# Column sums of the context added on the vector engine, and the order of three queues at the end of the first stage

## The chip, the cores and the metric

The kernel runs on one core of a Trainium2 chip. A core has a matrix engine (PE), a vector engine (DVE), a scalar engine (ACT), a general engine (POOL) and a queue that issues transfers (SP). Each runs its own list of instructions in order, and they wait for each other by semaphores. The metric is the time of one execution in microseconds (us) on the device; less is better.

## The reference, cut to what matters

Four steps update x (2 batches of 512 tokens, 1024 features): a product with the context, both operands rounded to 8 bits; an 8-bit feed-forward; an attention over the context; a 4-bit feed-forward. The change touches the first:

```python
def fake_quant(x, scale, zp):
    q = jnp.clip(jnp.round(x / s + z), QMIN, QMAX)
    return (q - z) * s
q1 = fake_quant(x1, x1_scale, x1_zp)
q2 = fake_quant(x2, x2_scale, x2_zp)
return jnp.matmul(q1, q2)
...
x = x + jnp.tanh(g_xattn[0]) * _L0_xattn_ref(_layernorm(x, axis=-1), ctx_4096, ...)
```

The zero points make a product with a correction: since q1 - z1 = u + (128 - z1), where u is what the kernel multiplies, the result is u times the rounded context, plus (128 - z1) times the sum of the rounded context over its 1024 tokens, for each feature (the column sums), plus a term for each token.

## The kernel before

**Stage 1** (to about 109 us) works through the 16 context tiles (128 tokens by 1024 features), in four chunks of four. Each tile is split in two fp16 halves, turned, and multiplied with Wk and Wv (v_proj, k_proj on PE). The raw tile is also scaled and clipped on POOL (ctx_affine) and rounded by DVE into `r2[:, u, :]` (ctx_round, L1043), integers in fp16 in the tile regR. In between DVE scales the eight rows of the int32 weight (wd_scale, L1049), PE turns them (wd_turn, L1463), ACT and DVE evict them in two halves (wd_high L690, wd_low L1036). The LayerNorm of x goes tile by tile (t = 0 to 7) from chunk 1 on: stats (L1058) and ln1_affine (L1065 to L1111, eight operations on two elements a partition) on DVE, a square root (L695) and the affine into `y` (L702) on ACT, ln1_round (L1115) on DVE, ln1_out (L709) on ACT, a turning transfer xt1 (L283) from SP into `xT_hi`.

**Column sums.** After the last k_proj and the turn of weight row 7, `c2_sum(n)` multiplies `ones16` with the eight rounded tiles of batch n // 2, 512 columns at a time: four sums of eight products (L1545), into bank n. ACT evicts each (c2_out, L743), and POOL adds the row to each tile of x (add_c2, L510). add_c2(0) waits for two evictions; add_c2(1) also waits until all eight roundings ln1_round are done (`ln1_q` = 8). POOL then goes on with the low halves of Wq (split_lo, L521 and L523), the bias (L530) and so on. SP loads the next row of Wq into `wraw` when such a low half is done; ACT makes the high half (wq_high, L843).

**The A/B stage** (116 to 200 us): for each tile of x the A product (16 products of 512 columns, L1612) and the B product (32, L1615 and L1616), in the order of `AB_OPS`: a0 to a4, b0, a5, b1, a6, b2, a7, b3 to b7. Three pairs of banks turn; product i waits until DVE has evicted product i - 3 (ab_out, L1216). The second, a1, also waits for `k_lo`, the low half of the last K block (k_low on DVE, L1119, behind k_out on ACT, L716), whose bank it takes. After A of a tile DVE takes the statistics, ACT the deviation from the mean (ln2_deviation, L812), DVE the largest absolute value (ln2_reduce, L1232), ACT scales and rounds (L817, L825), DVE clips (ln2_clip, L1254).

The order of each queue is written out by hand; the block of each engine is one list. `d()` is a drain on DVE: the next instruction starts when what is before it has ended.

## Time and profile before

| | us |
|---|---|
| median of 3 runs | 847.38 |
| lowest and highest | 844.66, 848.0 |
| the profiled execution | 841.13 |
| its span in the trace | 839.3 |
| PE, DVE, ACT, POOL busy | 818.1, 583.8, 449.6, 535.6 |

The profiled execution is one run of its own. The page has the busy time of each engine, the span in 40 slices, the DMA queues, the chain of work that ended last, and the costliest groups of instructions. In the rows below, L1043 is line 1043 of the kernel before. A row of an engine in order of time gives start and duration in us, engine, line, operation, output and input tiles (buffer numbers left out; mpair and sbank are banks of the accumulation memory), shapes, how many in a row, and in brackets the idle time before it and what ended it. PE's granted clock is 1.00 in all stretches used here, the higher of its two levels.

### The profile page before, as it was taken

How to read it: one execution, taken by the hardware profiler on the slowest of the kernel's cores; microseconds unless marked ns; L12 is line 12 of the kernel's file. 1: busy time of each engine (PE TensorE's matmuls, PEld its weight loads, DVE VectorE, ACT ScalarE, POOL GpSimd, SP SyncE). 2: the span in 40 equal slices, each digit the busy share in tenths (PEclk: the TensorE clock that was granted, in tenths of full speed). 3: DMA queues.
4: the chain of work that ended last, by engine and by line, in shares of the span. 5: the costliest groups of instructions: out<-in, count | busy, mean ns of one | idle time of the engine just before them, and what ended most of it. 6: DMA issues, size and time to landing. Idle time of an engine off the chain costs nothing.

```text
span 839.3 us, 14044 instructions
## 1 busy us (share of the span) xinstructions
PE 818.1 (97%) x4498; PEld 330.3 (39%) x4498; DVE 583.8 (70%) x855; ACT 449.6 (54%) x743; POOL 535.6 (64%) x235
## 2 busy tenths in 40 slices
PE   8999899999999999999999999999999879999998
PEld 7666644444444422222222222222222213444443
DVE  6888778885668677888888888888888401555522
ACT  5435477476221177777777777777777771112200
POOL 6745159958333367898888898888898884222300
PEclk9999999999999999999999999999999999999999
DMA  7999973439975124654554644554653543122341
GB/s 255 252 280 286 257 182 88 101 79 211 246 173 165 49 73 111 136 117 99 107 117 104 135 110 108 102 116 103 135 116 70 101 82 70 26 50 50 62 138 75
DMA packets 120822, 107.81 MB, mean 128 GB/s; under 512 B 85324, under 2 KB 105804, under 8 KB 116684
## 3 DMA queue, kind: packets, MB, share of 16 engines
q1 hardware_dynamic: 115120, 71.59, 33.3%
q0 software_dynamic: 4608, 33.56, 19.8%
q10 hardware_dynamic: 1052, 2.10, 0.8%
q8 instruction: 27, 0.44, 0.2%
q14 instruction: 15, 0.12, 0.0%
HBM read 41.55 MB, written 12.58 MB: 64 GB/s over the span
## 4 chain that ended last, share of the span: by engine, by line
PE 73%; POOL 8%; DMA 7%; issue 4%; DVE 4%; ACT 1%; DVEq 1%; ACTq 0%; POOLq 0%; SPq 0%
PE sbank L1691 10%; PE sbank L1702 10%; PE mpair L1631 10%; POOL wraw L608 6%; DMA tail<-wraw 5%; PE sbank L1492 4%; PE sbank L1491 4%; PE sbank L1490 4%; PE sbank L1769 3%; PE sbank L1786 3%; PE sbank L1771 3%; PE sbank L1784 3%; PE sbank L1773 3%; PE sbank L1712 2%; PE mpair L1615 2%
## 5 line engine op out<-in xcount | busy, mean ns | idle before, releaser
L1352 DVE TENSOR_REDUCE mx<-mpair 128x1 f32<-128x1024 f32 x256 | 302.3, 1217 | 59.6 <-PE mpair L1631 58.7
L913 ACT ACTIVATE regC<-sbank 128x512 f32<-128x512 f32 x512 | 277.9, 594 | 104.7 <-PE sbank L1691 100.9
L1691 PE MATMUL sbank<-regD 98*128 98x512 f16 x512 | 178.2, 384 | 6.6 <-ACT regC L913 5.6
L608 POOL TENSOR_TENSOR wraw<-regC 128x2048 f32<-128x2048 f32 x32 | 148.6, 4643 | 28.8 <-DMA tail<-wraw 25.5
L1631 PE MATMUL mpair<-regD 96*128 96x512 f16 x512 | 155.9, 380 | 1.1 <-DVE mx L1352 0.5
L1702 PE MATMUL sbank<-regC,regD 128*32 128x512 f32 x1024 | 136.4, 605 | 1.0 <-ACT regC L913 1.0
L1691 PEld LDWEIGHTS sbank<-regD 98*128 98x128 f16 x512 | 48.5, 97 | 184.8 <-ACT regC L913 147.3
L608 POOL TENSOR_TENSOR regD<-regC 128x2048 f32<-128x2048 f32 x16 | 75.7, 4729 | 14.9 <-ACT regC L913 14.9
L608 POOL TENSOR_TENSOR tail<-regC 128x2048 f32<-128x2048 f32 x16 | 76.8, 4799 | 0.1
L1631 PEld LDWEIGHTS mpair<-regD 96*128 96x128 f16 x512 | 47.6, 98 | 54.5 <-DVE mx L1352 13.9
L499 POOL TENSOR_SCALAR xT_lo<-xT_lo,sc 128x1024 f32<-128x1024 f32 x16 | 33.1, 2068 | 34.6 <-DVE bb L1111 14.7
L646 POOL TENSOR_TENSOR tail<-y,r 128x1024 f16<-128x1024 f32 x8 | 17.1, 2132 | 55.8 <-ACT r L954 55.8
L1769 PE MATMUL sbank<-regR,xT_hi 128*128 128x512 f16 x128 | 48.5, 379 | 0.0
L1771 PE MATMUL sbank<-regR,xT_hi 128*128 128x512 f16 x128 | 48.5, 379 | 0.0
L1773 PE MATMUL sbank<-regR,xT_lo 128*128 128x512 f16 x128 | 48.5, 379 | 0.0
L1784 PE MATMUL sbank<-regK,xT_hi 128*128 128x512 f16 x128 | 48.5, 379 | 0.0
L1786 PE MATMUL sbank<-regK,xT_lo 128*128 128x512 f16 x128 | 48.5, 379 | 0.0
L1490 PE MATMUL sbank<-xT_hi,regC 128*128 128x512 f16 x128 | 48.5, 379 | 0.0
L1492 PE MATMUL sbank<-xT_hi,regC 128*128 128x512 f16 x128 | 48.5, 379 | 0.0
L1491 PE MATMUL sbank<-xT_lo,regC 128*128 128x512 f16 x128 | 48.5, 379 | 0.0
L521 POOL TENSOR_SCALAR wraw<-wraw 128x1024 f32<-128x1024 f32 x16 | 17.2, 1073 | 47.0 <-ACT regR L850 46.9
L1425 DVE SCALAR_TENSOR_TENSOR X<-sbank,sc,X 128x512 f32 (+1 forms) x16 | 12.0, 749 | 50.0 <-PE sbank L1773 50.0
(193 smaller groups left out, 1266.4 us busy)
## 6 DMA issues: line engine op xcount, KB each, us to landing
regD<-wraw POOLq DMA_DIRECT2D x16, 1024.0 KB, 7.0
tail<-wraw POOLq DMA_DIRECT2D x16, 1024.0 KB, 7.0
xT_lo<-in_ctx SPq DMA_DIRECT2D x16, 512.0 KB, 4.9
wraw<-in_L_ffn_W_int SPq DMA_DIRECT2D x8, 512.0 KB, 4.5
X<-in_x SPq DMA_DIRECT2D x4, 1024.0 KB, 6.4
wraw<-in_L_xattn_Wq SPq DMA_DIRECT2D x8, 512.0 KB, 3.7
wraw<-in_L_xattn_Wo SPq DMA_DIRECT2D x8, 512.0 KB, 4.1
regD<-q_hi_scratch SPq DMA_DIRECT2D x32, 128.0 KB, 2.4
```

The source lines that it names most:

```text
L608: nc.gpsimd.tensor_tensor(p_sum[pr if pr < 3 else 1][:, :, :], probs[:, (2 * pr) % 4, :, :], probs[:, (2 * pr) % 4 + 1, :, :], ALU.add).th ...
L913: nc.scalar.activation(probs[:, kt % 4, h, :], bank[4 + h % 2], ACT.Exp, scale=SCALE).then_inc(s["exp_ok"], 1)
L1352: v.tensor_reduce(mx[m][:, bass.ds(n, 1)] if par is not None else mx[m][:, n:n + 1], slot[:, :, :], AX.XY, ALU.max).then_inc(s["mx_red"], 1)
L1490: pe.matmul(dst, whi(k), xhi(k), start=(k == 0), stop=False)
L1491: pe.matmul(dst, whi(k), xlo(k), start=False, stop=False)
L1492: m = pe.matmul(dst, wlo(k), xhi(k), start=False, stop=(k == KD - 1))
L1631: m = pe.matmul(mpair[slot][:, half, :], qst[par][0:96, bass.ds(n * P, P)], kst[par][0:96, half * 512:(half + 1) * 512], start=True, stop= ...
L1691: pe.matmul(bank[4 + h % 2], kst[par][0:98, kt * P:(kt + 1) * P], qst[par][0:98, h * 512:(h + 1) * 512], start=True, stop=True).then_inc(s ...
L1702: m = pe.matmul(bank[6][HD * h:HD * h + HD, :], vst[par][:, kt * HD:(kt + 1) * HD], probs[:, kt % 4, h, :], start=(kt == 0), stop=(kt == K ...
L1769: pe.matmul(bank[4 + h], xT_hi[:, k, bass.ts(t, P)], wo_hi[:, k, h * H2:(h + 1) * H2], start=(k == 0), stop=False)
L1771: pe.matmul(bank[4 + h], xT_hi[:, k, bass.ts(t, P)], wo_lo[:, k, h * H2:(h + 1) * H2], start=False, stop=False)
L1773: m = pe.matmul(bank[4 + h], xTl[:, k, bass.ts(t, P)], wo_hi[:, k, h * H2:(h + 1) * H2], start=False, stop=(k == KD - 1))
```

## The change

- `add_column(u)`, new, on DVE: it adds the rounded tile u to a running sum of its batch in fp16. The sums `col_sum[b]` lie in `xT_hi`, in the columns of x tiles 6 and 7. Fourteen additions (1 to 7 and 9 to 15; 1 and 9 add two rounded tiles), each behind a drain; the last of a batch counts `cs_ok` up.
- `c2_sum(n)` is one product of 512 columns, and waits for `cs_ok`. The four stand ahead of the turn of weight row 7.
- SP: the turning transfers of x tiles 6 and 7 wait until the four sums are made, since they write where `col_sum` lies.
- ACT: the sums 0 and 1 are evicted right behind the first half of the last K block, 2 and 3 behind the second half; both were behind the affine of tile 6 and at the end.
- POOL: the wait for all eight roundings moves from tile 1 to tile 2.
- DVE: `ln1_round(7)` and `wd_low(7)` move behind the eviction and the statistics of A tile 0.

```diff
--- before.py
+++ after.py
@@ -151,6 +151,7 @@
         wk_hi, wk_lo, wv_hi, wv_lo = [regK[:, 2048 * i:2048 * (i + 1)].rearrange("p (k n) -> p k n", k=KD)
                                       for i in range(4)]
 
+        col_sum = [xT_hi[:, 4 * b:4 * b + 4, (T - 2) * P:T * P] for b in range(B)]
         dev = [cx[:, 2 + i, :] for i in range(2)]
         Y3_HI = [0, 1, 2, 3, 14, 8, 9, 10]
         Y3_LO = [4, 5, 6, 7, 15, 11, 12, 13]
@@ -185,7 +186,7 @@
             ctx_tr ct_hi ct_lo ctx_hi ctx_lo cth0 cth1 ctl0 ctl1 cq_pool cq_done
             wd_prod wd_tr wd_hi_ok wd_lo_ok
             kv_mm k_hi k_lo v_ev k_st v_st
-            ln1_stat ln1_sd ln1_aff ln1_u ln1_q ln1_ready xt1_ev0 xt1_ev1 c1_ok x_c1 c2_mm c2_ev x_c2
+            ln1_stat ln1_sd ln1_aff ln1_u ln1_q ln1_ready xt1_ev0 xt1_ev1 c1_ok x_c1 cs_ok c2_mm c2_ev x_c2
             ab_mm ab_ev
             ln2_stat ln2_dev ln2_inv ln2_q ln2_ready ln2_sd xt2_ev0 xt2_ev1 bias_add
             ln3_stat ln3_sd ln3_aff y3_ok y3_hi y3_lo xt3a_hi xt3a_lo xt3b_hi xt3b_lo xt3c_hi xt3c_lo
@@ -349,6 +350,7 @@
             xt1(T - 4)
             xt1(T - 3)
             after_wd(7)
+            sp.wait_ge(s["c2_mm"], 2 * B)
             xt1(T - 2)
             xt1(T - 1)
             sp.dma_start(scale4[:, :, :], scales4.rearrange("(w p) b -> p w b", p=P)).then_inc(s["sc4_in"], 16)
@@ -505,7 +507,7 @@
                 if t % TB == 0:
                     pool.wait_ge(s["c2_ev"], 2 * (t // TB) + 2)
                 pool.wait_ge(s["ln1_u"], t + 1)
-                if t == 1:
+                if t == 2:
                     pool.wait_ge(s["ln1_q"], T)
                 nc.gpsimd.tensor_tensor(X[:, t, :], X[:, t, :], c2[:, t // TB, :], ALU.add).then_inc(s["x_c2"], 1)
 
@@ -795,17 +797,17 @@
             ln1_affine(T - 3)
             ln1_root(c)
             k_out(c, 0, False)
-            ln1_out(T - 3)
-            k_out(c, 1, False)
-            ln1_affine(T - 2)
             c2_out(0)
             c2_out(1)
+            ln1_out(T - 3)
+            ln1_affine(T - 2)
+            k_out(c, 1, False)
+            c2_out(2)
+            c2_out(3)
             ln1_out(T - 2)
             ln1_affine(T - 1)
             wd_high(T - 1)
             ln1_out(T - 1)
-            c2_out(2)
-            c2_out(3)
 
             def ln2_deviation(t):
                 act.wait_ge(s["ln2_stat"], t + 1)
@@ -1043,6 +1045,14 @@
                 v.tensor_scalar(r2[:, u, :], cx[:, u % TB, :], MAGIC, MAGIC + ZC, ALU.add,
                                 ALU.subtract).then_inc(s["cq_done"], 1)
 
+            def add_column(u):
+                b, n = u // KD, u % KD
+                d()
+                first = r2[:, u - 1, :].rearrange("p (k n) -> p k n", k=4) if n == 1 else col_sum[b]
+                ins = v.tensor_tensor(col_sum[b], first, r2[:, u, :].rearrange("p (k n) -> p k n", k=4), ALU.add)
+                if n == KD - 1:
+                    ins.then_inc(s["cs_ok"], 1)
+
             def wd_scale(w):
 
                 dve.wait_ge(win[w % 2], 16 * (w // 2 + 1))
@@ -1170,6 +1180,9 @@
                 ctx_round(u + 1)
                 dve.wait_ge(x_in[c - 1], 16)
                 stats(2 * c - 2, 2 * c - 2)
+                if c == 1:
+                    add_column(1)
+                    add_column(2)
                 k_low(c, 0)
                 wd_low(2 * c + 1)
                 ctx_low(u + 3)
@@ -1177,6 +1190,8 @@
                 d()
                 ln1_affine(c - 1)
                 ctx_round(u + 2)
+                if c == 2:
+                    add_column(5)
                 ln1_round(2 * c - 2)
                 wd_scale(2 * c + 2)
                 if u + TB < U:
@@ -1184,25 +1199,31 @@
                 k_low(c, 1)
                 ln1_round(2 * c - 1)
                 ctx_round(u + 3)
+                for n in ((3, 4), (6, 7))[c - 1]:
+                    add_column(n)
                 d()
 
             first_chunk()
             for c in range(1, NCH - 1):
                 chunk(c)
             c = NCH - 1
+            add_column(9)
+            add_column(10)
             wd_low(T - 2)
             wd_scale(T - 1)
             ln1_stats(c - 1)
             ln1_affine(c - 1)
+            add_column(11)
+            add_column(12)
             ln1_round(T - 4)
             ln1_stats(c)
+            for n in range(13, U):
+                add_column(n)
             ln1_round(T - 3)
             ln1_affine(c)
             k_low(c, 0)
             k_low(c, 1)
             ln1_round(T - 2)
-            ln1_round(T - 1)
-            wd_low(T - 1)
 
             def ab_out(i):
                 kind, t = AB_OPS[i]
@@ -1286,6 +1307,8 @@
 
             a_out(0)
             a_stats(0)
+            ln1_round(T - 1)
+            wd_low(T - 1)
             a_out(1)
             ln2_reduce(0)
             a_stats(1)
@@ -1538,14 +1561,11 @@
 
             def c2_sum(n):
 
-                if n == 0:
-                    pe.wait_ge(s["cq_done"], U)
+                pe.wait_ge(s["cs_ok"], n // 2 + 1)
                 pe.wait_ge(s["v_ev"], U - TB + n + 1)
-                for k in range(KD):
-                    m = pe.matmul(bank[n], ones16[:, :],
-                                  r2[:, KD * (n // 2) + k, (n % 2) * H2:(n % 2 + 1) * H2], start=(k == 0),
-                                  stop=(k == KD - 1))
-                m.then_inc(s["c2_mm"], 1)
+                pe.matmul(bank[n].rearrange("p (k n) -> p k n", k=2), ones16[:, :],
+                          col_sum[n // 2][:, 2 * (n % 2):2 * (n % 2) + 2, :], start=True,
+                          stop=True).then_inc(s["c2_mm"], 1)
 
             def idle_products(n):
 
@@ -1586,9 +1606,9 @@
                 if not last:
                     wd_turn(2 * c + 1)
                 k_proj(c, 1)
-            wd_turn(KD - 1)
             for n in range(2 * B):
                 c2_sum(n)
+            wd_turn(KD - 1)
 
             def stage_ab(i):
                 kind, t = AB_OPS[i]
```

The orders below give line, operation, tiles, shape and what an instruction waits for. Line numbers of the changed kernel are up to 21 higher than before: L1052 is the new addition, L1075 to L1121 ln1_affine, L1125 ln1_round, L1129 k_low, L1237 the eviction of an A or B product.

DVE from the last statistics of stage 1 on, before:

```order
L1060 BN_AGGR mv<-stt 128x2
L1115 TENSOR_SCALAR y<-y 128x1024 [waits ln1_u]
L1065 TENSOR_SCALAR nhalf<-mv 128x2
L1067 RECIPROCAL rr<-sd 128x2 [waits ln1_sd]
L1069 TENSOR_TENSOR ra<-rr 128x2
L1071 TENSOR_TENSOR ra<-ra,nhalf 128x2
```

and in the changed kernel:

```order
L1070 BN_AGGR mv<-stt 128x2
L1052 TENSOR_TENSOR xT_hi<-xT_hi,regR 128x4x256 x3
L1125 TENSOR_SCALAR y<-y 128x1024 [waits ln1_u]
L1075 TENSOR_SCALAR nhalf<-mv 128x2
L1077 RECIPROCAL rr<-sd 128x2 [waits ln1_sd]
L1079 TENSOR_TENSOR ra<-rr 128x2
L1081 TENSOR_TENSOR ra<-ra,nhalf 128x2
```

Three additions stand between the statistics of x tiles 6 and 7 and the rounding of tile 5 (L1125), and ln1_affine(3) follows that.

DVE a little later, from the last k_low to the first reduction, before:

```order
L1119 SCALAR_TENSOR_TENSOR tail<-sbank,tail 128x512 [waits k_hi] x2
L1115 TENSOR_SCALAR y<-y 128x1024 [waits ln1_u] x2
L1036 TENSOR_TENSOR regD<-sbank,regD 128x4x128 [waits wd_hi_ok] x2
L1216 SCALAR_TENSOR_TENSOR X<-mpair,sc,X 128x512 [waits ab_mm,x_c2]
L1216 SCALAR_TENSOR_TENSOR X<-mpair,sc,X 128x512 [waits ab_mm]
L1058 BN_STATS stt<-X 128x6 x2
L1060 BN_AGGR mv<-stt 128x2
L1216 SCALAR_TENSOR_TENSOR X<-sbank,sc,X 128x512 [waits ab_mm,x_c2]
L1216 SCALAR_TENSOR_TENSOR X<-sbank,sc,X 128x512 [waits ab_mm]
L1232 TENSOR_REDUCE sbank<-xT_lo 128x1 [waits ln2_dev]
```

and in the changed kernel:

```order
L1129 SCALAR_TENSOR_TENSOR tail<-sbank,tail 128x512 [waits k_hi] x2
L1125 TENSOR_SCALAR y<-y 128x1024 [waits ln1_u]
L1237 SCALAR_TENSOR_TENSOR X<-mpair,sc,X 128x512 [waits ab_mm,x_c2]
L1237 SCALAR_TENSOR_TENSOR X<-mpair,sc,X 128x512 [waits ab_mm]
L1068 BN_STATS stt<-X 128x6 x2
L1070 BN_AGGR mv<-stt 128x2
L1125 TENSOR_SCALAR y<-y 128x1024 [waits ln1_u]
L1038 TENSOR_TENSOR regD<-sbank,regD 128x4x128 [waits wd_hi_ok] x2
L1237 SCALAR_TENSOR_TENSOR X<-sbank,sc,X 128x512 [waits ab_mm,x_c2]
L1237 SCALAR_TENSOR_TENSOR X<-sbank,sc,X 128x512 [waits ab_mm]
L1253 TENSOR_REDUCE sbank<-xT_lo 128x1 [waits ln2_dev]
```

One rounding and the eviction of weight row 7 moved from ahead of the first A tile's eviction to behind its statistics.

ACT from the eviction of the last K block's first half (L716 with sbank0), behind the last square root of stage 1, before:

```order
L716 ACTIVATE tail<-sbank0 128x512 [waits kv_mm,k_st]
L709 ACTIVATE tail,c1<-y,sc 128x1024 [waits xt1_ev1,ln1_q]
L716 ACTIVATE tail<-sbank1 128x512 [waits kv_mm,k_st]
L702 ACTIVATE y<-X,bb,rr 128x1024 [waits ln1_aff]
L743 ACTIVATE xT_lo<-mpair0,sc 128x512 [waits c2_mm,consts_ok]
L743 ACTIVATE xT_lo<-mpair0,sc 128x512 [waits c2_mm]
L709 ACTIVATE r16,c1<-y,sc 128x1024 [waits xt1_ev0,ln1_q]
L702 ACTIVATE y<-X,bb,rr 128x1024 [waits ln1_aff]
L690 ACTIVATE regD<-sbank2 128x4x128 [waits wd_tr]
L690 ACTIVATE regD<-sbank3 128x4x128 [waits wd_tr]
L709 ACTIVATE tail,c1<-y,sc 128x1024 [waits xt1_ev1,ln1_q]
L743 ACTIVATE xT_lo<-mpair1,sc 128x512 [waits c2_mm] x2
```

and in the changed kernel:

```order
L718 ACTIVATE tail<-sbank0 128x512 [waits kv_mm,k_st]
L745 ACTIVATE xT_lo<-mpair0,sc 128x512 [waits c2_mm,consts_ok]
L745 ACTIVATE xT_lo<-mpair0,sc 128x512 [waits c2_mm]
L711 ACTIVATE tail,c1<-y,sc 128x1024 [waits xt1_ev1,ln1_q]
L704 ACTIVATE y<-X,bb,rr 128x1024 [waits ln1_aff]
L718 ACTIVATE tail<-sbank1 128x512 [waits kv_mm,k_st]
L745 ACTIVATE xT_lo<-mpair1,sc 128x512 [waits c2_mm] x2
L711 ACTIVATE r16,c1<-y,sc 128x1024 [waits xt1_ev0,ln1_q]
L704 ACTIVATE y<-X,bb,rr 128x1024 [waits ln1_aff]
```

The evictions of the sums (L743, L745) moved ahead: two of them are now ahead of the output of tile 5, and the second half of K (sbank1) is behind the affine of tile 6.

POOL, the additions to x, before:

```order
L510 TENSOR_TENSOR X<-X,xT_lo 128x1024 [waits ln1_u,c2_ev]
L510 TENSOR_TENSOR X<-X,xT_lo 128x1024 [waits ln1_q,ln1_u]
L510 TENSOR_TENSOR X<-X,xT_lo 128x1024 [waits ln1_u] x2
```

and in the changed kernel:

```order
L512 TENSOR_TENSOR X<-X,xT_lo 128x1024 [waits ln1_u,c2_ev]
L512 TENSOR_TENSOR X<-X,xT_lo 128x1024 [waits ln1_u]
L512 TENSOR_TENSOR X<-X,xT_lo 128x1024 [waits ln1_q,ln1_u]
L512 TENSOR_TENSOR X<-X,xT_lo 128x1024 [waits ln1_u]
```

The wait for `ln1_q` moved by one tile.

## Rows read from the trace of the kernel before

**Rows 1.** PE's waits, 56 to 270 us: who waited for whom: total, times, longest.

```profile
PE sbank L1463 <- DVE wraw L1049: 2.7, 1, 2.7
...
PE mpair L1612 <- DVE X L1216: 0.5, 1, 0.5
PE mpair L1631 <- DVE mx L1352: 0.5, 1, 0.5
```

**Rows 2.** Chain that ended last, 109 to 152 us: start, duration, what.

```profile
109.60 6.91 PE mpair L1545 x32
...
151.54 0.59 PE mpair L1612 x2
```

**Rows 3.** Busy time of each engine in one stretch: length, then engines.

```profile
124.00:152.00 28.00, 27.50 (x129) 12.30 (x127) 25.14 (x51) 17.38 (x17) 27.47 (x15) 1.00 0.39 100
```

**Rows 4.** PE in order of time: start, duration, what, idle before.

```profile
108.56 1.04 PE L1463 MATMUL sbank<-id,wraw 128*128 128x128 f32 x8
```

**Rows 5.** DVE in order of time, 93 to 125 us.

```profile
93.74 0.69 DVE L1043 TENSOR_SCALAR regR<-xT_lo 128x1024 f16<-128x1024 f32 x1
96.16 1.29 DVE L1036 TENSOR_TENSOR regD<-sbank,regD 128x512 f16<-128x512 f32 x2 [1.74 <-ACT regD L690]
...
104.95 0.69 DVE L1115 TENSOR_SCALAR y<-y 128x1024 f32<-128x1024 f32 x1 [1.37 <-ACT y L702]
...
108.35 0.21 DVE L1060 BATCH_NORM_AGGREGATE mv<-stt 128x2 f32<-128x12 f32 x1
...
116.27 0.69 DVE L1115 TENSOR_SCALAR y<-y 128x1024 f32<-128x1024 f32 x1 [3.11 <-ACT y L702]
...
123.45 0.75 DVE L1216 SCALAR_TENSOR_TENSOR X<-sbank,sc,X 128x512 f32<-128x512 f32 x1 [0.40 <-PE sbank L1612]
124.30 1.23 DVE L1232 TENSOR_REDUCE sbank<-xT_lo 128x1 f32<-128x1024 f32 x1
```

**Rows 6.** DVE in order of time: three operations that price one.

```profile
57.79 1.23 DVE L1023 TENSOR_TENSOR X<-xT_lo,X 128x1024 f16<-128x1024 f32 x1
...
102.10 0.16 DVE L1069 TENSOR_TENSOR ra<-rr 128x2 f32<-128x2 f32 x1
...
156.60 0.37 DVE L1254 TENSOR_SCALAR r<-r 128x1024 f16<-128x1024 f16 x1
```

**Rows 7.** All engines in order of time, 55 to 92 us: three rows.

```profile
55.87 0.69 DVE L1119 SCALAR_TENSOR_TENSOR tail<-sbank,tail 128x512 f16<-128x512 f32 x1 [0.47 <-ACT tail L716]
...
89.62 1.28 POOL L501 TENSOR_SCALAR xT_lo<-xT_lo 128x1024 f32<-128x1024 f32 x1 [0.15 <-issue]
89.94 2.04 DVE L1049 SCALAR_TENSOR_TENSOR wraw<-wraw,wscale 128x1024 f32<-128x1024 int32 x1
```

**Rows 8.** POOL in order of time, 113 to 127 us.

```profile
113.86 2.36 POOL L510 TENSOR_TENSOR X<-X,xT_lo 128x1024 f32<-128x1024 f32 x1 [22.96 <-ACT xT_lo L743]
117.11 9.31 POOL L510 TENSOR_TENSOR X<-X,xT_lo 128x1024 f32<-128x1024 f32 x4 [0.88 <-DVE y L1115]
```

**Rows 9.** POOL and DVE in order of time where they meet.

```profile
40.55 3.20 POOL L499 TENSOR_SCALAR xT_lo<-xT_lo,sc 128x1024 f32<-128x1024 f32 x1
...
42.77 0.99 DVE L991 TENSOR_TENSOR sc<-sc 128x1 f32<-128x1 f32 x1
...
140.40 2.38 POOL L510 TENSOR_TENSOR X<-X,xT_lo 128x1024 f32<-128x1024 f32 x1
...
141.40 1.66 DVE L1254 TENSOR_SCALAR r<-r 128x1024 f16<-128x1024 f16 x1
```

**Rows 10.** ACT in order of time, 111 to 157 us.

```profile
111.19 1.24 ACT L702 ACTIVATE y<-X,bb,rr 128x1024 f32<-128x1024 f32 x1
112.34 1.45 ACT L743 ACTIVATE xT_lo<-mpair,sc 128x512 f32<-128x512 f32 x2
...
152.47 1.06 ACT L843 ACTIVATE regC<-wraw 128x1024 f16<-128x1024 f32 x1 [4.01 <-DMA wraw<-in_L_xattn_Wq]
...
156.71 1.15 ACT L812 ACTIVATE xT_lo<-X,mv 128x1024 f32<-128x1024 f32 x1 [0.83 <-DVE mv L1060]
```

## The prediction

> **What bounds the kernel now.** I read the page first: PE is busy for 97% of the span, so I looked for what makes it wait. The list of PE's waits between 56 and 270 us [rows 1] is short: 2.7 us at the turn of weight row 6, which waits for DVE's scaling (L1049), 0.5 us in the A/B stage, which waits for DVE's eviction (L1216), and 0.5 us in the Q stage, at 253 us; two more are below 1 us each. From 92.04 to 151 us PE streams without a gap, and in that stretch lie the 32 products of the column sums: 6.91 us on the chain of waits [rows 2]. On paper these are the prize.
>
> The chain tells where the prize would go. It does not stay on PE: from the second A tile's eviction at 123.45 us it runs over DVE up to 151.54 us, where PE is released [rows 2]. DVE is busy for 25.1 of the 28 us from 124 to 152 [rows 3]. So an earlier start on PE is worth only as much as DVE's step at 124.30 us, the first reduction of the row maxima (L1232), comes earlier [rows 5]. The question of this case is when that step starts.
>
> **PE's part.** 28 products less at 6.91/32 = 0.216 us make 6.05 us. PE is done with the last K product at 108.7 us [rows 4]. The sums of batch 1, though, now wait for `cs_ok`, that is for DVE's last addition; behind them in PE's queue stand the last weight turn and the first A tile.
>
> **Price of one addition.** The trace has no DVE operation with two 16-bit inputs. Nearest rows: 1024 elements from two inputs, one of them f32, take 1.23 us; one 16-bit input takes 0.37 us when POOL is out of the way [rows 6]. An f32 one-input operation of 1024 elements takes 0.69 us [rows 5], so halving the width of what is read halves a one-input time, but for a fixed part of about 0.16 us (the length of the two-element operations [rows 6]). The same step on 1.23 us gives (1.23 - 0.16)/2 + 0.16 = 0.70 us. I take 0.69 plus 0.08 us for the drain before each (the gap between drained small operations), 0.77 us; the bounds are 0.37 + 0.08 = 0.45 and 1.23 + 0.08 = 1.31 us. The Trainium skill ("VectorE: DVE Perf Modes", the perf-mode tier table) gives `tensor_tensor` in bf16 from SBUF its two-element mode, which is what I took.
>
> **Additions 1 to 5.** 1 and 2 fall on an idle of 0.47 us ahead of 55.87 us [rows 7]: DVE runs 1.54 - 0.47 = 1.1 us late. SP's load of context tile 15 waits for a rounding that comes 1.1 us later. The DMA engines were fully busy then, so I let 0.4 us of it through (bounds 0 and 1.1). 3 and 4 fall in an idle that is longer than both, where DVE waits for ACT's copy of context tile 13, and are free. Addition 5 stands ahead of `ln1_round(2)` and of the scaling of weight row 6, the DVE step that PE waits 2.7 us for [rows 1, 7]. A short idle is there, but POOL works in it, and both engines seem to queue for something: `wd_scale` took 2.04 us, until 1.08 us after POOL's L501 had ended [rows 7]. So addition 5 counts in full, 0.75 us. PE's wait grows by 0.75 + 0.4 = 1.15 us: the K products end at 109.9 us instead of 108.73.
>
> **Additions 6 to 15.** DVE ends its last rounding of context at 94.4 us [rows 5] and I take it 1.5 us later (0.4 and 0.75 as above, and 0.35 for ACT, which takes its turn between `ln1_round(2)` and `(3)` later; bounds 1.0 and 2.5). 6, 7, 9, 10 cost 3.1 us on an idle of 1.74 us, 1.35 us more. 11 and 12 cost 1.54 us on 1.37 us, 0.15 more. The statistics of chunk 3 end at 108.56 us before [rows 5], so T = 108.56 + 1.5 + 1.35 + 0.15 = 111.5 us. 13 to 15 follow: `cs_ok` is complete at T + 2.4 = 113.9 us. PE stands still from 110.3 to 113.9 us; the sums of batch 1 take 0.4 and the weight turn 0.9 us [rows 4]; the first A tile starts at 115.2 instead of 116.5 us. Of 6.05 us 1.3 are left on PE.
>
> **The steps that the change moves.** ACT now evicts column sums 0 and 1 right behind the first K eviction, all of it after the square root that T releases: 0.3 + 0.6 + 1.3 us [rows 10], so `c2_ev` is 2 at T + 2.2 us. POOL's add_c2(0) starts there, and add_c2(1) follows at once, since the wait for all roundings (`ln1_q` = 8) was moved from tile 1 to tile 2. Before, add_c2(0) ran from 113.86 us in a time when DVE was idle for 3.11 us, and tiles 1 to 4 started only behind the last rounding (0.88 us of waiting) [rows 5, 8]. Now both, 2.33 us each, fall on `ln1_round(5)` and `ln1_affine(3)`.
>
> What a POOL operation does to such a DVE operation is in the trace: the clip of 0.37 us that started at 141.40, inside POOL's L510 from 140.40 to 142.78 us, took 1.66 us, until 0.28 us after POOL's end. A DVE operation on a single element with two SBUF inputs (L991) took 0.99 us, to the end of POOL's L499 at 43.75 us; it takes 0.16 us elsewhere [rows 6, 9]. And where both engines had their next operation ready, they took turns: `wd_scale` went on only behind L501, which itself had waited for DVE's rounding [rows 7]. The Trainium skill says the same ("SBUF — State Buffer", Who interferes with whom): the shared port pair is an exclusive lock for a whole instruction, for DVE operations in the two-port modes or with two SBUF inputs. By that rule the trace agrees, 1.66 and 0.99 us.
>
> So: POOL takes add_c2(0) until T + 4.7; `ln1_round(5)` ends at T + 5.3; add_c2(1) then runs until T + 7.6, and the two-input steps of `ln1_affine(3)` (L1069, L1071) wait for it. It ends at T + 9.2 us. ACT's affine of tile 6 (1.2 us [rows 10]) and behind it the second K eviction (0.6), now in that order, give k_low at T + 11.7; the second A tile on PE waits for `k_lo` until then. `ln1_round(6)` 0.6, a_out(0) 1.4, its statistics 1.5, `ln1_round(7)` 0.6, wd_low(7) 1.2 and a_out(1) 1.4 us bring DVE to T + 18.4. The deviation that L1232 reads comes from ACT, where ln1_out(7) (which waits for the moved rounding), a weight copy and the deviation itself need 1.2 + 1.1 + 1.1 us: T + 19.3 = 130.8 us. Before it was 124.30 us [rows 5]: **+6.5 us**.
>
> POOL's third addition waits for `ln1_round(7)`: 127.3 us instead of 119.4, +7.9 us [rows 8]. POOL has no gap from 117.11 until after 150 us, so its low half of Wq row 2 moves by 7.9 us, and with it the load that ACT waited 4.01 us for at 152.47 us. ACT has 0.83 us of slack behind it [rows 8, 10]. So the stage ends 7.9 - 0.8 = **+7.1 us**. From 151.54 to 253.20 us PE never waits [rows 1], so what is late there stays late.
>
> **Sum.** 841.13 us (profiled execution; span 839.3) + 7 = 848.1. The median of the runs is 847.38, 6.3 above the profiled one; on it the forecast is 854.4, I say 854. With T between 111.0 and 112.5 us (from the bounds of the shift at 94.4 us) it is 853.9 to 855.4, and with one collision fewer or more, 2.3 us, 851.6 to 857.7.
>
> **The rivals.**
> - *The small operations do not wait* (or POOL's additions start after them). Only the 2.3 us for one rounding, or nothing, is lost. Without any of it DVE's step is at +2.2 us (T + 15.0), POOL at +3.9, and the stage ends at +3.1 us: 850.5. For it: of small operations the rows show L991 alone waiting. Chance 0.22.
> - *DVE absorbs all* (faster, the other side). Between 94.4 and 124.3 us DVE's four longest idles come to 1.74 + 1.37 + 3.11 + 0.40 = 6.6 us [rows 5], the nine additions 6, 7 and 9 to 15 cost 6.9. If they fell into the idle, and PE's lead carried through, L1232 would come as early as ACT allows: 1 to 6 us off, 841.4 to 846.4, typically 844. It decides for the gain if `cs_ok` is complete before PE has ended its K products. Against it: of the idle 3.11 us lies behind the additions, where it can't be used by them. Chance 0.12.
> - *The addition runs at one element per cycle*, 1.31 us: nine times 0.54 is 4.9 us more, of which 0.7 are in idle time, and 0.54 at addition 5: about +12, 859. Chance 0.08.
> - *The change does little*: PE's waits and DVE's move against each other and the sum is within 1 us of nothing, 847. Chance 0.08.
>
> **How the numbers follow.** Forecast 0.50 at 854. Range: from 846 (half of the third rival's 0.12 is below, some 0.08) to 859.5 (half of the slow addition is above, and 0.04 for a collision worse than thought); that leaves out less than 0.2. Half a per cent, about what a measurement of this kernel can tell from no change, is 4.2 us: slower by more are the forecast and the slow addition, 0.58; within it the first and the last rival and half a tenth of the gain, 0.34; faster 0.08.
>
> **What would show it.** Right: POOL's first two X additions back to back over `ln1_round(5)`, which takes some 3 us instead of 0.69, and an `ln1_affine(3)` with one small step of about 2 us; PE's wait for `cs_ok` 3 to 4 us; a wait of the second A tile for `k_lo`; L1232 first at about 130 us; ACT's wait for the Wq load above 4 us. Wrong: L1232 first before 125 us, or additions of another length than 0.69 us. The weakest steps are T, in which 2 us of shift through ACT and SP are estimated, and who gets its turn first.

## Result and profile after

The changed kernel takes **851.57 us** (median of 13 runs, 848.38 to 853.67), the kernel before on the same chip **844.66 us** (13 runs, 840.82 to 849.25). The ratio is **1.007, 95% interval 1.0049 to 1.0092**: 6.9 us slower. The profiled execution took 853.28 us with a span of 851.5 us.

Three traces of each kernel were taken in all (the later ones are the runs r1 to r4 below). Four moments carry the comparison: the start of DVE's 16th and last low half of a context tile (`ctx_low`, L1023 before, L1025 after); T, the end of the last statistics of chunk 3; the start of the first row maximum (L1232 before, L1253 after), on which the prediction hung the stage; and the end of the span.

| us | 16th low half | T | first row maximum | span |
|---|---|---|---|---|
| before, three traces | 83.02, 83.12, 81.59 | 108.56, 108.67, 107.14 | 124.30, 126.09, 122.89 | 839.3, 841.9, 839.0 |
| after, three traces | 86.97, 87.96, 87.00 | 115.71, 116.71, 115.75 | 134.67, 135.66, 134.71 | 851.5, 851.6, 851.2 |
| difference of the means | +4.7 | +7.9 | +10.6 | +11.4 |

The forecast was 854 us and +7. Its 854 stood on a median of 847.38 us from three runs of before; the 13 runs gave 844.66.

From the first row maximum to the end of the span it is 715.0 to 716.1 us before and 715.9 to 716.8 us after. So nearly all that was lost was lost in the first 135 us: 4.7 us ahead of the last low half, 3.2 between it and T, 2.7 between T and the row maximum.

PE's waits in the changed kernel, 56 to 290 us (who waited for whom, total, times, longest), which answer to [rows 1]:

```profile
PE sbank L1486 <- DVE wraw L1059: 6.7, 1, 6.7
PE sbank L1632 <- DVE tail L1129: 4.2, 1, 4.2
PE mpair L1566 <- DVE xT_hi L1052: 3.1, 1, 3.1
PE sbank L1486 <- DVE regC L1032: 2.2, 1, 2.2
```

The wait for the scaled weight row has grown from 2.7 to 6.7 us, and two waits are new: the sums of batch 1 stand 3.1 us for DVE's additions (L1052), and the second A tile stands 4.2 us for the low half of K (L1129). The four products are indeed all that is left of 32. PE in order of time (start, duration, engine, line, what, times, idle before):

```profile
114.44 0.59 PE L1566 MATMUL mpair<-xT_hi,ones 128*128 128x512 f16 x2
118.13 0.60 PE L1566 MATMUL mpair<-xT_hi,ones 128*128 128x512 f16 x2 [3.10 <-DVE xT_hi L1052]
118.58 1.04 PE L1486 MATMUL sbank<-id,wraw 128*128 128x128 f32 x8
119.45 3.62 PE L1632 MATMUL mpair<-regR,xT_hi 128*128 128x512 f16 x16
127.30 4.97 PE L1632 MATMUL sbank<-regR,xT_hi 128*128 128x512 f16 x16 [4.23 <-DVE tail L1129]
```

DVE in order of time, from the last addition to the first row maximum; this is [rows 5] of after:

```profile
115.50 0.21 DVE L1070 BATCH_NORM_AGGREGATE mv<-stt 128x2 f32<-128x12 f32 x1
115.85 2.23 DVE L1052 TENSOR_TENSOR xT_hi<-xT_hi,regR 128x1024 f16<-128x1024 f16 x3
118.00 2.84 DVE L1125 TENSOR_SCALAR y<-y 128x1024 f32<-128x1024 f32 x1
120.76 2.32 DVE L1075 TENSOR_SCALAR nhalf<-mv 128x2 f32<-128x2 f32 x1
122.99 0.15 DVE L1077 RECIPROCAL rr<-sd 128x2 f32<-128x2 f32 x1
...
126.55 0.69 DVE L1129 SCALAR_TENSOR_TENSOR tail<-sbank,tail 128x512 f16<-128x512 f32 x1 [1.25 <-ACT tail L718]
...
132.49 1.40 DVE L1237 SCALAR_TENSOR_TENSOR X<-sbank,sc,X 128x512 f32<-128x512 f32 x2
134.67 1.23 DVE L1253 TENSOR_REDUCE sbank<-xT_lo 128x1 f32<-128x1024 f32 x1 [0.78 <-ACT xT_lo L814]
```

T is 115.50 + 0.21 = 115.71 us. Behind the three additions stands the collision that the prediction described: a rounding of 2.84 us instead of 0.69, and one step on two elements that takes 2.32 us instead of 0.17. POOL in order of time shows the other party, its two additions on X back to back, and its third; this is [rows 8] of after:

```profile
117.76 5.29 POOL L512 TENSOR_TENSOR X<-X,xT_lo 128x1024 f32<-128x1024 f32 x2 [22.91 <-ACT xT_lo L745]
...
131.52 7.01 POOL L512 TENSOR_TENSOR X<-X,xT_lo 128x1024 f32<-128x1024 f32 x3 [8.46 <-DVE y L1125]
```

POOL then has the end: the chain of waits runs over POOL from 133.64 us to the load of Wq, for which ACT waits 6.35 us where it waited 4.01 [rows 10]. The chain, then ACT in order of time:

```profile
133.64 2.56 POOLq L524
136.20 2.32 POOL X L512
...
158.18 2.14 POOL regC L525
160.33 3.86 DMA wraw<-in_L_xattn_Wq
164.22 1.06 ACT regC L845
...
164.22 1.06 ACT L845 ACTIVATE regC<-wraw 128x1024 f16<-128x1024 f32 x1 [6.35 <-DMA wraw<-in_L_xattn_Wq]
```

### The profile page after: what moved, and what is told of

Its sections match the earlier page's. It is cut to its first block, busy times and chain, and to the rows that moved or that the text cites. A ratio compares the mean times of both kernels' runs of the same rounds, so it can differ in the third digit from the quotient of the medians.

```text
span 851.5 us, 14020 instructions
## 1 busy us (share of the span) xinstructions
PE 816.0 (96%) x4470; PEld 329.4 (39%) x4470; DVE 598.7 (70%) x869; ACT 449.5 (53%) x743; POOL 535.7 (63%) x235
## 4 chain that ended last, share of the span: by engine, by line
PE 73%; DVE 7%; DMA 5%; POOL 3%; ACT 3%; SPq 3%; issue 2%; DVEq 2%; POOLq 1%; ACTq 1%
PE sbank L1722 14%; PE sbank L1711 14%; PE mpair L1651 12%; PE sbank L1789 3%; PE sbank L1806 3%; PE sbank L1793 3%; PE sbank L1804 3%; PE sbank L1791 3%; PE sbank L1732 3%; PE sbank L1513 3%; PE sbank L1515 3%; PE sbank L1514 3%; DVEq L973 2%; PE mpair L1635 2%; PE mpair L1636 2%
```

## Experiments

Kernels of one group ran on one chip and share its runs of the kernel before: 843.8 us for e1 to e4, 844.41 us for e5 to e8. What is compared across groups is the distance to that: the changed kernel's is +6.9 us. The theory: additions ahead of T make T late by about their own time, and behind T POOL's two early additions on X collide with DVE. The rivals: PE's longer wait for the weight row (6.7 us) is what counts; or the moved order is the whole loss.

**e1: the collision taken away.** The changed kernel; POOL's first two additions on X wait until DVE is through.

```diff
+                if t == 0:
+                    pool.wait_ge(s["ln1_aff"], NCH)
+                if t == 1:
+                    pool.wait_ge(s["ln1_q"], T - 1)
```

> The changed kernel with two waits of POOL set so that its first two additions to x meet no DVE operation that needs the shared port: add_c2(0) also waits for the last ln1_affine, add_c2(1) for seven roundings. In the changed kernel's profile ln1_round(5) took 2.84 us instead of 0.69 and the first step of ln1_affine(3) 2.32 instead of 0.17, and the first ln2_reduce came 18.96 us after T (the end of the last statistics of stage 1). Theory (the collision is part of the loss): both are short again, ln2_reduce at T + 15, the kernel 3 to 4.5 us faster than the changed one, so 2 to 4 us over the kernel before. Rival (DVE would have waited there for ACT or PE anyway): T + 19 as before, no difference from the changed kernel, 7 us over the kernel before.

Measured 846.9 us (845.51 to 849.86), ratio to before 1.004 (1.0026 to 1.0055): +3.1 us. Its trace, DVE in order of time behind the additions, with T at 116.58 + 0.21 = 116.79 us:

```profile
116.58 0.21 DVE L1074 BATCH_NORM_AGGREGATE mv<-stt 128x2 f32<-128x12 f32 x1
...
119.07 0.69 DVE L1129 TENSOR_SCALAR y<-y 128x1024 f32<-128x1024 f32 x1
...
131.74 1.23 DVE L1257 TENSOR_REDUCE sbank<-xT_lo 128x1 f32<-128x1024 f32 x1 [0.78 <-ACT xT_lo L818]
```

The rounding is back at 0.69 us, and from T to the row maximum it is 14.95 us against 18.96. The collision costs 4.0 us in the trace and 3.8 in the medians (6.9 - 3.1). Part of the 3.8 may be PE's clock: seven of the 12 runs had a mean granted clock of 0.996, which no run of the changed kernel had (0.990 to 0.994); the other five have a median of 848.02 us, +4.2, which leaves 2.7 for the gate. PE still waited 6.9 us for the weight row here, so that wait is not what separates this kernel from the changed one.

**e2: additions and four products, in the old order** of ACT, POOL, DVE and PE behind T.

```diff
-                if t == 2:
+                if t == 1:
                     pool.wait_ge(s["ln1_q"], T)
...
+            ln1_out(T - 3)
+            k_out(c, 1, False)
+            ln1_affine(T - 2)
             c2_out(0)
             c2_out(1)
-            ln1_out(T - 3)
-            ln1_affine(T - 2)
-            k_out(c, 1, False)
-            c2_out(2)
-            c2_out(3)
...
```

What the diff leaves out puts back `c2_out(2)` and `(3)`, the places of `ln1_round(7)` and `wd_low(7)`, and the turn of weight row 7 ahead of the sums.

> The additions and the four products of the changed kernel, with ACT, POOL, DVE and PE otherwise in the order of the kernel before (sum evictions, the wait for all roundings at tile 1, ln1_round(7) and wd_low(7) ahead of the first A tile, weight row 7 turned ahead of the sums). Theory (T is late by the additions and that is most of the loss): T near 115.7 us as in the changed kernel, ln1_affine(3) without a long step, ln2_reduce at T + 17 to 18; 5 to 8 us over the kernel before. Rival (the loss is the moved order): within 1.5 us of the kernel before.

Measured 849.04 us (847.73 to 850.55), ratio 1.0053 (1.0033 to 1.0072): +5.2 us, as expected. T is 115.71 us, as in the changed kernel; T to the row maximum is 17.39 us, 1.65 more than before; the steps of `ln1_affine(3)` take 0.16 to 0.23 us each, and POOL's first addition starts only at 122.99 us. The first A tile on PE, here and before:

```profile
122.97 5.80 PE L1632 MATMUL mpair<-regR,xT_hi 128*128 128x512 f16 x16 [4.22 <-ACT xT_lo L745]
...
116.34 3.62 PE L1612 MATMUL mpair<-regR,xT_hi 128*128 128x512 f16 x16
```

With the sums made early, PE waits for ACT's evictions of them instead: the tile starts 7.26 us behind T, only half a microsecond sooner than the 7.78 of before. Its 16 products took 2.2 us longer, at a granted clock of 0.62 from 122.9 to 128.8 us, after PE had stood 1.87 and 4.22 us. DVE waits for PE 0.86 and 0.40 us in that stretch, so up to 1.3 of the 1.65 us are PE's slow products in this trace; how much of the +5.2 they make in the other runs is open.

**e3: the new order alone:** the kernel before, with 32 products and no additions, and the order of the changed kernel on all four engines.

```diff
-            ln1_out(T - 3)
-            k_out(c, 1, False)
-            ln1_affine(T - 2)
             c2_out(0)
             c2_out(1)
+            ln1_out(T - 3)
+            ln1_affine(T - 2)
+            k_out(c, 1, False)
+            c2_out(2)
+            c2_out(3)
...
```

> The kernel before with its 32 products and no addition, but with the moved order of ACT, POOL, DVE and PE. Theory: T as before, 108.5 us; the roundings are done before POOL starts except the one of tile 6; ln2_reduce 1 to 2 us later than the 124.30 of before, POOL 3 us later; 1 to 3 us over the kernel before. Rival (the moved order is the loss): 5 us or more over it.

Measured 847.84 us (845.11 to 850.02), ratio 1.0034 (1.0018 to 1.0049): +4.0 us, more than the theory had. ACT in order of time says why. Its evictions of the sums now stand ahead of the second K eviction (L716), and they wait for the 32 products:

```profile
116.42 0.69 ACT L743 ACTIVATE xT_lo<-mpair,sc 128x512 f32<-128x512 f32 x1 [3.84 <-PE mpair L1545]
118.09 0.69 ACT L743 ACTIVATE xT_lo<-mpair,sc 128x512 f32<-128x512 f32 x1 [0.98 <-PE mpair L1545]
...
121.14 0.57 ACT L716 ACTIVATE tail<-sbank 128x512 f16<-128x512 f32 x1
```

T to the row maximum is 20.36 us, 4.6 more than before. POOL's two additions run here from 118.86 to 123.53 us, and the rounding at 122.35 us took 1.73 us instead of 0.69, so about 1 us of it is a collision again. T was at 111.77 us and not at 108.5 as expected, 3.2 us late without a single addition (see r1 to r4). So the order needs the early column sums. The additions with the four products cost 5.2, the order alone 4.0, both together 6.9: with the sums ready early ACT's wait is gone and the full collision with POOL has come in its place.

**e4: the early additions moved** out of the places ahead of `k_low` and `wd_scale`: 1 and 2 to the end of chunk 1, 3 and 4 to the end of chunk 2, and 5, 6, 7, 9 and 10 together ahead of `wd_low(6)`.

```diff
-                if c == 1:
-                    add_column(1)
-                    add_column(2)
...
-                if c == 2:
-                    add_column(5)
...
-                for n in ((3, 4), (6, 7))[c - 1]:
+                for n in ((1, 2), (3, 4))[c - 1]:
...
-            add_column(9)
-            add_column(10)
+            for n in (5, 6, 7, 9, 10):
+                add_column(n)
```

> The changed kernel with additions 1, 2 and 5 out of the middle of chunks 1 and 2: 1 and 2 stand at the end of chunk 1, 3 and 4 at the end of chunk 2, 5, 6, 7, 9, 10 ahead of wd_low(6). Nothing else is moved. Theory (three additions in the middle of the chunks delay SP's queue and PE's weight turn): PE waits 2.7 us for weight row 6 as in the kernel before and not 6.7, the clock stays at its higher level, T at 112 to 113 us instead of 115.7, and 2.5 to 3.5 us faster than the changed kernel. Rival (the 6.7 us come of how transfers happened to fall): PE's wait stays above 5 us, T at 118 us, no faster than the changed kernel.

Measured 851.03 us (847.65 to 853.09), ratio 1.0074 (1.005 to 1.0098): +7.2 us, no gain over the changed kernel, a miss. PE's wait for the weight row did fall to 3.3 us. The 16th low half started at 84.76 us, 2.2 earlier, but from there to T, where additions 3 and 4 now stand as well, it was 29.61 us instead of 28.74, and T was 114.37 us. With T to the row maximum at 18.92 us the collision was whole. Of the 2.2 us, 0.9 was lost again ahead of T; the 1.3 us that were left in the trace don't show in the medians. PE's shorter wait for the weight row brought nothing there either.

**e5: early additions left out** (1 to 6, 9 and 10; the column sums are of fewer tiles).

```diff
-                first = r2[:, u - 1, :].rearrange("p (k n) -> p k n", k=4) if n == 1 else col_sum[b]
+                first = r2[:, u - 1, :].rearrange("p (k n) -> p k n", k=4) if u in (7, 11) else col_sum[b]
...
-                if c == 1:
-                    add_column(1)
-                    add_column(2)
...
-                if c == 2:
-                    add_column(5)
...
-                for n in ((3, 4), (6, 7))[c - 1]:
+                for n in ((), (7,))[c - 1]:
...
-            add_column(9)
-            add_column(10)
```

> The changed kernel without additions 1 to 6, 9 and 10 (the column sums are then of fewer tiles): 6 of 14 are left, one of them in chunk 2, five in the last stretch. Theory, the early additions shift the loads and stores of SP and the scales of the integer weights and so arrive at the end of the statistics (T, 115.71 us in the changed kernel, 108.56 before) with most of their own length: T = 108.56 + 3 additions of 0.77 = 110.9 if no transfer is late, the wait of PE for the weight scale at 96 us back from 6.7 to under 3.5 us, total 3.5 to 5 us under the changed kernel (846.5 to 848). The two-addition collision with POOL after T stays (steps of 2.3 to 2.8 us). Rival, the early additions lie in idle time of DVE and only the last stretch counts: T goes down by the two additions 9 and 10 alone (to about 114.2) and the total by 1.5 us, to 850.

Measured 847.09 us (845.91 to 850.81), ratio 1.0027 (1.0007 to 1.0047): +2.7 us, so 4.2 less than the changed kernel's 6.9, as the theory had it. T came at 113.08 us, not at 110.9, for this execution's 16th low half started at 87.47 us although no addition stood ahead of it. From there to T it was 25.61 us, with additions 7, 11 and 12 in between, against 25.54 before with none: these three, 2.3 us of work, fall into idle time and cost 0.07. The 3.2 us more of the changed kernel are then those of 5, 6, 9 and 10. The collision stayed, 18.91 us from T to the row maximum.

**e6: late additions left out** (11 to 14; fewer tiles here too).

```diff
-            add_column(11)
-            add_column(12)
...
-            for n in range(13, U):
+            for n in range(U - 1, U):
```

> The changed kernel without additions 11 to 14 (fewer tiles in the sums): what stands in the last stretch is 9, 10 and 15. Theory, in the last stretch DVE is never idle, so each addition costs its pitch of 0.77 us once: T goes down by 1.5 us (to 114.2), the one remaining addition after T ends 1.5 us sooner still, PE's sums start near 115 us, and the total goes down by 2.3 to 3.1 us, to 848.5 to 849.3. Rival, from T on POOL and the lock set the pace: the two additions of POOL still meet the rounding, T's 1.5 us is all that is gained, 850.

Measured 849.91 us (848.47 to 852.17), ratio 1.0067 (1.0044 to 1.0091): +5.5 us, 1.4 less than the changed kernel, which is the rival's number and not the theory's 2.3 to 3.1. Its reason is not the rival's, though. The trace has T at 113.14 us only because the 16th low half came at 84.48 us; from there to T it was 28.66 us against 28.74, so 11 and 12 cost nothing, as in e5. The row maximum comes 17.24 us behind T, 1.7 less than in the changed kernel, for two additions less behind T (1.54 us). The trace also shows which steps wait for POOL. POOL started at 115.19 us, and other small steps were hit:

```profile
114.49 0.16 DVE L1075 TENSOR_SCALAR nhalf<-mv 128x2 f32<-128x2 f32 x1
...
115.27 2.29 DVE L1083 SCALAR_TENSOR_TENSOR rr<-ra,rr 128x2 f32<-128x2 f32 x1
117.64 2.23 DVE L1116 TENSOR_SCALAR rr<-rr,sc 128x2 f32<-128x2 f32 x1
119.94 0.16 DVE L1118 SCALAR_TENSOR_TENSOR bb<-mv,rr 128x2 f32<-128x2 f32 x1
```

Each of POOL's two additions holds back one DVE step here, the one that stands next. L1075, which waited in the changed kernel, is free here, and L1116, a step with one tensor input, waits.

**e7: few sums.** The kernel before with additions 1 and 2 at the end of chunk 1, 3 and 4 at the end of chunk 2, and 24 products. It adds up into the first context tile itself, which the A products read later, so they compute something else here at the same cost.

```diff
...
-                for k in range(KD):
+                for k in range(KD) if n // 2 else (0, 5, 6, 7):
...
```

> The kernel before with four additions alone (1 and 2 at the end of chunk 1, 3 and 4 at the end of chunk 2) and 24 products in place of 32; its order is kept. The sums give PE 8 products of 0.216 us back, 1.7 us on its path to the first A tile. Theory, four additions of 0.77 us in chunks 1 and 2 pass on part of their 3.1 us as they did in the changed kernel: T = 109.5 to 110.3, total between 1 us faster and 1.5 us slower than before. Rival, at these two places they fall into idle time of DVE wholly: T unchanged, total 1.0 to 1.7 us faster.

Measured 842.72 us (840.78 to 847.25) against 844.41, ratio 0.9991 (0.997 to 1.0011): no difference that these runs can tell. T was 111.48 us, with the 16th low half at 85.60 us. From T to the row maximum it was 15.04 us against 15.74: of the 8 × 0.216 = 1.7 us that PE was spared, 0.7 arrived. The other 1.0 is not lost behind PE but ahead of its sums. These started 1.90 us behind T and not 0.88, for after a stop of 3.38 us the weight turn took 1.97 us instead of 1.09 and the first products behind it 0.42 instead of 0.27. From the first A tile on PE to the row maximum it is 7.96 us here and in all three traces of before, and DVE still waits for PE, 0.68 us at the second eviction. Close behind PE stands ACT: DVE's rounding of tile 6 waited 2.91 us for it, where it had waited 3.11 [rows 5]. The first A tile on PE and DVE's rows:

```profile
118.56 3.62 PE L1621 MATMUL mpair<-regR,xT_hi 128*128 128x512 f16 x16
...
118.99 0.69 DVE L1121 TENSOR_SCALAR y<-y 128x1024 f32<-128x1024 f32 x1 [2.91 <-ACT y L702]
...
122.22 0.75 DVE L1224 SCALAR_TENSOR_TENSOR X<-mpair,sc,X 128x512 f32<-128x512 f32 x1 [0.68 <-PE mpair L1621]
```

**e8: e1 and e4 together,** both diffs above in one kernel.

> Both earlier cures at once: additions 1 to 4 at the chunk ends, 5 to 7, 9, 10 after chunk 2, and POOL's first two additions held back until the affine steps and the rounding of DVE are over. Theory, the collision is worth its 4 us wherever T stands: T near 114.4, rounding 0.7 us and first affine step 0.16 us, total 846 to 847.5. Rival, the total is set by something that both leave alone (the clock of PE, the three POOL additions at 7 us): as with the gate alone at best, and the 1.3 us of the earlier T do not show, or the moved kernel's 851 stays above 849.

Measured 846.88 us (844.55 to 851.94), ratio 1.0032 (1.0008 to 1.0057). That is +2.5 us, where e4 had +7.2: the gate takes 4.7 us off it. T was at 114.72 us, the row maximum 15.34 us behind it. T is 2.1 us earlier than in e1, the distance to before 0.6 smaller, within what the two intervals leave open.

**r1 to r4: both kernels again,** two more traces of each. They were to tell whether the early additions make the 16th low half late or whether that moment wanders by itself.

> The kernel before once more, unchanged, for a second trace. The last low half of the context tiles (16th, L1023) started at 83.02 us in the first trace of before, at 86.97 in the changed kernel, but also at 86.23 and 87.47 in two kernels with no addition ahead of it (the order alone; the early additions left out). Theory A, the early additions push the loads of SP: before again at 82.5 to 84, end of the statistics T at 108 to 109.5. Theory B, the moment varies from execution to execution by itself, with the transfers: before again anywhere from 83 to 87.5, T = that moment + 25.5, the span 839 to 843 with it.

> The changed kernel once more, unchanged. Theory A: its 16th low half again at 86.5 to 87.5 us, T at 115.7. Theory B: anywhere from 84 to 88, T = that moment + 28.7. Under either, the steps after T repeat: rounding 2.8 us and one small step at 2.3 us beside POOL's two additions, first row maximum at T + 19.

> As for the second trace of before: theory A 82.5 to 84 us for the 16th low half, theory B spread over 83 to 87.5 us. From T to the first row maximum 15.7 us under both.

> As for the second trace of the changed kernel: theory A 86.5 to 87.5 us, theory B spread over 84 to 88 us; from T to the first row maximum 19 us under both.

Single executions of 843.75 and 840.82 us (before) and 853.48 and 853.09 us (after). At the 16th low half the two kernels stayed apart, 81.6 to 83.1 us and 87.0 to 88.0 us, which speaks for theory A. But e3 had the last low half at 86.23 us with no additions, and e5 at 87.47 us with none ahead of it, and e4, e6, e7 and e8, with two to four additions ahead of it, lay between 84.48 and 85.60; e1 and e2, with the four additions of the changed kernel ahead of it, had 88.05 and 86.96. Both theories fall as they were put. At the 15th low half the kernels are apart too (75.91, 75.53 and 73.98 us before; 77.26, 78.09 and 79.48 after), and again e3 and e5 lie between (76.11 and 77.05). The stretch from the 15th to the 16th took 7.1 to 7.9 us in six traces (the three of before, e4, e6 and the third of after) and 9.0 to 10.4 us in the other eight, with DVE waiting for a transfer in several of those (the low half behind `regC<-X`). What throws it is open.

The second trace of before shows one thing more. PE in order of time:

```profile
92.15 1.75 PE L1463 MATMUL sbank<-id,wraw 128*128 128x128 f32 x8 [2.99 <-DVE wraw L1049]
...
111.22 7.07 PE L1545 MATMUL mpair<-regR,ones 128*128 128x512 f16 x32
```

After 2.99 us of standing the weight turn took 1.75 us instead of 1.09, the first nine products behind it 0.42 instead of 0.27 us, and the sums started 1.8 us later than in the first trace (109.44 us). The rounding of tile 6 then waited 4.79 us, and the row maximum came 17.42 us behind T instead of 15.74. In all three traces of before the row maximum comes 7.96 us after PE starts the first A tile: in the kernel before PE is on the path there. In the changed kernel it is not: PE's wait for the weight row was 6.7, 6.9 and 3.2 us in its three traces, and T to the row maximum 18.96, 18.95 and 18.96.

## Why the prediction held, and where its steps did not

**The sign and the size held, and the mechanism in the main.** +7 us was forecast, +6.9 measured. The reason was to be that little of PE's saved time arrives while DVE's additions do, and that the moved evictions let POOL collide with DVE. The gate alone gives back 3.8 us (e1; 2.7 among runs of like clock), which shows the collision. The additions with the four products cost 5.2 (e2); there the first A tile starts only 0.5 us nearer to T, since it waits for ACT, and up to 1.3 us in its trace are slow products on PE, which the prediction did not have. So e2's 5.2 is not DVE's time alone.

**Price of one addition:** 0.69 us, in a row at a pitch of 0.77 (`x3` in 2.23 us). As predicted.

**The transfers' shift was mis-sized, and its cause is only half known.** The term was 0.4 us, with bounds 0 and 1.1. Chunk 1's `k_low` came 1.4 us later (57.32 us against 55.87 [rows 7]), and at the 16th low half the traces stood 3.95 us apart, 4.7 in the mean. The prediction let a delay die out in busy DMA engines; it grew. But e3 and e5 reached the same lateness, or nearly, without these additions, so not all of it can be booked on them.

**From there to T** the prediction had 0.75 + 0.35 + 1.35 + 0.15 = 2.6 us for seven additions; it was 3.2 in all three traces. The idles of DVE took 2.2 of their 5.4 us; 11 and 12 were free, as forecast (e6). T was forecast at 111.5 us and came at 115.71; of the 4.2 us missing, 3.55 are the transfers' term and 0.6 this one.

**From T on** the sum was nearly exact: 19.3 us to the row maximum forecast, 18.96 measured; the additions of POOL from T + 2.2 (measured 2.05), the third at T + 15.8 (measured 15.81), the low half of K at T + 11.7 (measured 10.84). Instead of 130.8 us the row maximum started at 134.67 only because T was late. One detail was wrong: not the steps with two inputs (L1079, L1081, which are L1069 and L1071 before) waited but L1075, with one tensor input on two elements. The Trainium skill ("SBUF — State Buffer", Who interferes with whom) lets a DVE operation compete for the shared port pair if it is in a two-port mode or has two SBUF inputs, counts `tensor_scalar` among those that can enter such a mode, and has the loser blocked for the whole instruction. The trace agrees that it is a whole instruction: each step that waits takes some 2.3 us, the length of one POOL addition. That `tensor_scalar` steps on two f32 elements wait as well, 2.32 us here and 2.23 at L1116 in e6, fits the page too; of the small steps the prediction had counted only those with two inputs. Whether these small steps really run in a two-port mode no run here tells.

**PE's wait for the weight row** was forecast at 2.7 + 1.15 us and was 6.7. It cost nothing that could be found: e4 has it at 3.3 us with the same median, the third trace of after at 3.2 with the same T and span.

**The rivals.** "The small operations do not wait" was refuted by the trace, but its number without any collision, 3.1 us over before, is what e1 measured when the gate took the collision away. As T came 4.2 us later than the sum had it, that agreement is luck in part too. "DVE absorbs all" failed where the prediction said: the idle of 3.11 us lies behind the additions.

**Part of the agreement of the total is luck.** In the traces the kernels lie 11.4 us apart, in the medians 6.9. The three profiled executions of before (841.13, 843.75 and 840.82 us) lie below its median of 844.66, those of after (853.28, 853.48, 853.09) above 851.57. The row maximum came 3.9 us later than forecast; with that the same sum gives +11, the distance of the traces and not of the medians.

PE's mean granted clock of each run says something more. Of the 55 runs of before beside e1 to e8, the eight with a mean clock of 1.000 took 840.86 to 842.18 us, the 24 with 0.996 or less 843.37 to 847.98. The three traces of before have 1.000, 0.998 and 1.000, so they and the prediction's sum are of its quick executions. The second one shows one way in which it gets slower: after a stop PE's products are slow, and PE is on the path. All 13 runs of the changed kernel have 0.990 to 0.994 and show no such split. So the plain runs of before give away a part of its lead, some 2 to 3 us from its quick runs to its median. That the clock is the cause in them is argued from one trace and not shown, since only profiled executions leave rows; why the three of after lie above their median stays open.

No version came out ahead of the kernel before. The best of the changed order are e8 and e1, 2.5 and 3.1 us behind it; e7 can't be told from it.

## What to carry over

Before giving PE's work to another engine, find who is late next once PE is done: here, with 6.05 us of products gone, the first A tile waited for ACT's evictions and started 0.5 us nearer to T (e2). What work on an engine with idles costs depends on the place: three additions fell into idle time and cost 0.07 us of 2.3, four others cost 3.2 (e5). And when an edit makes a result ready earlier, look at which engine it wakes and what that one locks: two POOL operations that started 2 us after T instead of behind the last rounding cost 3.8 of the 6.9 us.

## What the runs showed of the hardware

- The step that loses against POOL can be as small as two elements with one tensor input: 2.32 us instead of 0.17. Two POOL additions in a row cost DVE two waits, one each, with the first held step done between them (L1125 and L1075 in the changed kernel, L1079 and L1081 in e5, L1083 and L1116 in e6). Not every step is held: in e3 the low half of K, with one input from a bank, took its usual 0.69 us at 121.74 us beside a POOL addition, and the rounding behind it 1.73.
- 1024 elements from two fp16 inputs into fp16 took 0.69 us, as long as one f32 input in place; with a POOL operation beside it the same addition took 1.51 us (at 92.44 us).
- The granted clock of PE was 1.00 from 84 to 110 us in the first and third trace of before and 0.93 in the second, though PE stood 2.7, 3.4 and 3.0 us there. In the changed kernel it was 0.87, 0.87 and 0.93 after 6.7, 6.9 and 3.2 us. In the second trace of before the first nine products of 256 columns behind the stop took 0.42 us each, the granted clock from 92.15 to 95.8 us being 0.54; two more took 0.38 and 0.28 and the later ones 0.27 us: 1.2 GHz, then 2.4.
